# A two-layer graph network on one core: indirect gathers and adding scatters without an upper bound for their indices

## The reference

```
edge_index = jnp.stack([src, dst])        # dst sorted; layer 1: row = src, col = dst
h = jnp.maximum(_layernorm(x), 0.0)
# layer 0
g = (h @ W_embed).reshape(n, H, D)
z = dot(g, a_src)[src] + dot(g, a_dst)[dst];  logit = leaky_relu(z, 0.2)
prob = segment_softmax(logit, dst)
x = x + segment_sum(g[src] * prob, dst) + h @ W_lin + bias
h = jnp.maximum(_layernorm(x), 0.0)
# layer 1
m = relu(concat(h[row], h[col], edge_attr) @ W1 + b1) @ W2 + b2
x = x + h + segment_sum(m * sigmoid(edge_attr @ Wa + ba), row)
```

## Time and profile before

| | |
|---|---|
| median of three runs | 1527.07 us (1523.6 to 1528.55) |
| the profiled execution | 1523.76 us |
| its span in the trace | 1522.0 us |
| GpSimd busy | 1137.3 us, 75% |
| VectorE busy | 1103.2 us, 72% |
| TensorE busy | 1022.8 us, 67% |
| ScalarE busy | 781.4 us, 51% |

### The profile page before, as it was taken

One profiled execution on the slowest core, in us unless ns is written; L12 is line 12 of the kernel. 1 busy time (PEld: TensorE's weight loads), 2 busy tenths in 40 slices (PEclk: granted clock), 3 DMA queues, 4 the chain that ended last, 5 costly groups with the idle time before them and its releaser, 6 DMA issues.

```text
span 1522.0 us, 21349 instructions
## 1 busy us (share of the span) xinstructions
PE 1022.8 (67%) x5699; PEld 766.9 (50%) x5699; DVE 1103.2 (72%) x3789; ACT 781.4 (51%) x2168; POOL 1137.3 (75%) x992
## 2 busy tenths in 40 slices
PE   0877777777778854665554577767777667767774
PEld 0666555555556644555544354544544444445543
DVE  3889898988889897988888655555555555555562
ACT  0788888888888885665665322222222222222221
POOL 5777777777777703777777778888888888888885
PEclk9999999999999986667686688899889889898898
DMA  8477777767677753565554333333333333333332
GB/s 274 124 225 216 223 226 212 241 212 229 211 227 218 219 201 106 178 186 166 171 179 154 102 46 51 51 53 51 50 51 51 53 50 47 52 51 51 51 41 26
DMA packets 177732, 202.55 MB, mean 133 GB/s; under 512 B 22191, under 2 KB 130739, under 8 KB 177483
## 3 DMA queue, kind: packets, MB, share of 16 engines
q1 hardware_dynamic: 119305, 122.62, 25.2%
q0 software_dynamic: 56496, 71.62, 23.7%
q10 hardware_dynamic: 1810, 6.93, 1.3%
HBM read 90.62 MB, written 109.66 MB: 132 GB/s over the span
## 4 chain that ended last, share of the span: by engine, by line
POOL 44%; issue 26%; DMA 16%; DVE 6%; PE 4%; ACT 2%; POOLq 0%; DVEq 0%; ACTq 0%
POOL out_dram L1166 16%; POOL XE L1151 7%; DMA out_dram<-BD,sx 7%; POOL R L434 4%; POOL XN L434 4%; POOL O L434 4%; POOL out_dram L1107 4%; POOL XE L434 4%; DMA XE<-out_dram,ixs 2%; DMA XE<-in_x_dram 2%; DMA out_dram<-BS,sx 1%; DMA out_dram<-BD 1%; DMA O<-in_x_dram,ix 1%; DMA XE<-in_x_dram,ix 1%; DVE H L879 1%
## 5 line engine op out<-in xcount | busy, mean ns | idle before, releaser
L1107 POOL DMA_INDIRECT out_dram<-BD,sx x196 | 206.3, 1053 | 114.1 <-issue 59.4
L1151 POOL DMA_INDIRECT XE<-out_dram,ixs x196 | 210.5, 1074 | 61.8 <-issue 56.7
L1280 DVE TENSOR_SCALAR XN<-bank,bwc 128x128 f32<-128x128 f32 x196 | 55.2, 344 | 260.6 <-PE bank L1420 260.6
L705 ACT ACTIVATE BD<-BD,nmr,rstd 128x128 f32<-128x128 f32 x392 | 170.9, 489 | 63.3 <-DVE nmr L565 63.3
L1046 PE MATMUL bank<-BD 128*128 128x128 f32 x392 | 111.0, 378 | 123.4 <-DVE BD L924 123.4
L1166 POOL DMA_INDIRECT out_dram<-BS,sx x100 | 160.0, 1600 | 37.3 <-issue 33.7
L1166 POOL DMA_INDIRECT out_dram<-TS,sx x96 | 153.1, 1595 | 34.8 <-issue 28.8
L1399 PE MATMUL bank<-ident,XE 128*128 128x128 f32 x196 | 40.9, 344 | 179.5 <-DMA XE<-out_dram,ixs 179.5
L1046 PEld LDWEIGHTS bank<-BD 128*128 128x128 f32 x392 | 87.7, 276 | 134.0 <-issue 134.0
L779 PE MATMUL bank<-wes,TS 128*128 128x132 f32 x392 | 101.3, 342 | 79.3 <-ACT TS L716 78.9
L767 PE MATMUL bank<-ident,BD 128*128 128x128 f32 x588 | 106.3, 292 | 71.7 <-DVE BD L558 69.7
(11 more groups left out here) (238 smaller groups left out, 3222.1 us busy)
## 6 DMA issues: line engine op xcount, KB each, us to landing
out_dram<-BD SPq DMA_DIRECT2D x96, 512.0 KB, 3.1
base_rows<-BD SPq DMA_DIRECT2D x49, 256.0 KB, 4.4
BD<-base_rows SPq DMA_DIRECT2D x49, 256.0 KB, 3.4
H<-BD SPq DMA_DIRECT2D x49, 256.0 KB, 3.0
XE<-in_x_dram SPq DMA_DIRECT2D x13, 512.0 KB
BD<-bond_rows SPq DMA_DIRECT2D x49, 128.0 KB, 2.1
bond_rows<-in_edge_attr_dram ACTq DMA_DIRECT2D x1, 6250.0 KB, 23.5
XN<-in_x_dram SPq DMA_DIRECT2D x12, 512.0 KB
```

What stands on the lines that cost most here:

```text
L705: last = nc.scalar.activation(OT[u][:, g, w:w + D], OT[u][:, g, w + D:w + 2 * D], ACT.Relu, bias=nmr[:, slot, t:t + 1], scale=rstd[:, slot ...
L1107: pool.indirect_dma_start(out, bass.IndirectOffsetOnAxis(sx[:, u, c:c + 1], 0), RO4[u][:, c, :], None, bounds_check=lim, oob_is_err=False) ...
L1151: pool.indirect_dma_start(XS4[u][:, c, :], None, halves, bass.IndirectOffsetOnAxis(ixs[:, u, c:c + 1], 0), bounds_check=lim, oob_is_err=Fa ...
L1280: last = nc.vector.tensor_scalar(MS[:, c * D:(c + 1) * D], bM[:, c * D:(c + 1) * D], bwc[:, u % 2, c:c + 1], None, ALU.mult)
```

## The change

The bound is taken from three kinds of indirect DMA: the gathers of layer 0, the fetches of layer 1 and the adding scatters. Two registers are then no longer filled. The plain scatters keep the bound. Lines behind the first edit move up by one, behind the second by two (L434 becomes L433, L1107 becomes L1106, L1151 becomes L1149 and L1166 becomes L1164).

```diff
         def rows_gpsimd(pool):
-            lim = pool.to_reg(N - 1)
...
                         pool.indirect_dma_start(XA[u][:, c, SRC - s, :], None, x, bass.IndirectOffsetOnAxis(at, 0),
-                                                bounds_check=lim, oob_is_err=False).then_inc(ld_xe[u][c], 16)
+                                                bounds_check=None, oob_is_err=False).then_inc(ld_xe[u][c], 16)
...
         def messages_gpsimd(pool):
-            lim = pool.to_reg(2 * ROWS_OUT - 1)
 
             def fetch(u, c):
                 pool.indirect_dma_start(XS4[u][:, c, :], None, halves, bass.IndirectOffsetOnAxis(ixs[:, u, c:c + 1], 0),
-                                        bounds_check=lim, oob_is_err=False).then_inc(ld_s[u], 16)
+                                        bounds_check=None, oob_is_err=False).then_inc(ld_s[u], 16)
...
                                                 UPD[u][:, c * D:(c + 1) * D], None,
-                                                bounds_check=lim, oob_is_err=True, compute_op=ALU.add).then_inc(ms_add, 16)
+                                                bounds_check=None, oob_is_err=True, compute_op=ALU.add).then_inc(ms_add, 16)
```

## The result

The changed kernel takes 1502.82 us (median of 4 runs, 1502.1 to 1505.48) against 1526.61 us for the kernel before (median of 4 runs, 1523.6 to 1528.55). The ratio is 0.9846, with a 95% interval from 0.9827 to 0.9864. That is faster by 23.8 us, where 53.5 had been forecast. The profiled execution has a span of 1501.1 us, 20.9 less than before; the stages are compared in it.

What follows compares the result with a forecast made beforehand. POOL, issuing indirect DMAs without pause in layer 0 and the messages, was taken as the bound. Savings of 27.4 + 0 + 25.8 + 0.3 = 53.5 us gave 1473 us at the median, range 1420 to 1531 (8 in 10).

Steps and rivals of the forecast that it cites:

- the cover: Layer 0: DVE's floor of 9.3 us a tile lies below POOL's shortened 9.9 us, so POOL's saving shows in the span.
- the first term of the sum: Layer 0: 392 gathers, each 0.07 us shorter without the bound, give 27.4 us.
- The price d: Time of the bound check inside one indirect DMA: 0.07 us likeliest, 0.13 us the end of the likely span.
- Messages: 368 x 0.07 = 25.8 us: Layer 1 messages: 368 adds and fetches on POOL, each 0.07 us shorter, give 25.8 us.
- The copy's loop: Messages: fetched rows through PE to ACT's update copy, which the add needs; 1.7 us of slack per turn of eight DMAs.
- The landing's loop: Messages: an add pair waits until the pair before has landed, 3.24 us after its start; 1.2 us in hand.
- the first fetches: Four fetches of the first batch, on whose landing the first add waits: 0.3 us gained.
- Zero terms: No gain from plain scatters, which keep their bound, or the final drain of 12 adds; the 54.7 us wait before the scatters stays.
- The free check (1): Rival: the check costs nothing in any of the indirect DMAs, time 1524 to 1527 us; chance 0.27.
- The dear check (2): Rival: the check costs 0.15 us or more per indirect DMA, 1415 us at 0.15, not below 1393; chance 0.09.
- A cost of a change of form (3): Rival: the unbounded form costs POOL extra on 764 DMAs, 1555 us at 0.04 us each, 1585 at 0.08; chance 0.06.
- Signs foretold: Profile after: layer 0 step 1.24 us, fetches 0.97 to 1.01, adds 1.50 to 1.55, last gather about 510, messages turn 12.6.

## Why the prediction was right or wrong, point by point

**What bounds the kernel.** POOL, from the first gather to the last fetch: right for the chip of the first measurement. There the gathers' stretch followed their spans with little loss, and the cover was there as said: between 100 and 500 us DVE still waited 29 us for gathered rows, 40 before. It was a reading of one chip at a granted clock of 0.96; at 0.80 POOL waits for DVE and DVE for TensorE, and the first term of the sum is worth nothing.

**The price d.** An eighth of the extra work of an add, 0.07 us, was a guess between 0 and 0.57. Measured it is 0.052 for a gather and 0.067 for a fetch; that the guess came so near for these two is luck, since no row priced a check. Of the 27.4 us for layer 0, 20.4 were there and 17.5 came, since the gathers had more long ones among them (13.4 us instead of 9.3). The direction held and this term was too large by 10 us.

**The adds.** This is the step that failed: "Messages: 368 x 0.07 = 25.8 us". Half of these 368 instructions are adds, and their bound costs nothing, in the changed kernel, alone, and in either mode. That takes 12.9 us off. The prediction had put one d on all three kinds of instruction, though it had just used the add to show that its time is made of something else. No row of the trace could tell what a bound costs in an add, and no reason was given why it should cost the same there.

**The slack.** The two loops that might take the gain away were the right ones, but the slack was read from a single turn. The copy's loop was given 1.7 us, from a turn of the middle class in which the add followed 2.03 us behind the copy, less 0.3. But no add that waited follows its copy by less than 0.83 us, so that turn had 1.2, and the turns of the slow class, 0.85 to 0.95 behind, had about 0.1. The landing's loop was given 1.2 us with the same 0.3; with 0.83 it had 0.7, and the landing of an add does not take 3.24 us each time. The trace of the kernel before already had 7 turns in which POOL waited for landings of 3.8 to 4.0 us, and in the changed one two took over 5. Of 12.3 us that the fetches saved, 4.4 reached the stretch. That is the second failed step, 7.9 us; waits of POOL make 5.5 of them, and most of the rest are the longer first adds, for which the prediction had no term and the runs show no cause.

**The sum.** From 53.5 to 21.0 us of span 32.5 are missing: 9.9 in layer 0, 12.9 for the adds, 0.6 for the size of d in the fetches, 7.9 in the turns, 0.3 for the first fetches, and 0.9 net in between (a later start and a longer wait for DVE, less a shorter way from the first scatter to the first add).

**Zero terms.** The plain scatters stayed at 0.985 us in the median, as a control should; the wait ahead of them stayed at 55 us (56.1); the drain gave nothing.

**The rivals.** The free check (1) is what the adds have, and not the gathers. Of the rule of the Trainium skill, page "DMA: Bandwidth & Descriptors", section "Anatomy of one DMA — SWDGE (gpsimd) path", that the generation of descriptors is small beside about 2 us of fixed cost: in these traces POOL is held for 0.95 to 1.08 us by a gather or fetch, and the landing of a fetch comes at 2.7 us. The trace agrees that the larger part of the latency is elsewhere. It does not follow that less time on POOL is worth nothing, since POOL issues these DMAs one behind the other. The dear check (2) is refuted, 0.05 to 0.07 instead of 0.15. A cost of a change of form (3) is at most 0.008 to 0.009 us where bounded and unbounded gathers alternate, and it has no part in this change, nor is the unbounded form slower; that a fetch behind an add takes 0.05 us more than the next one is as before (1.02 and 0.97 now), and belongs to the operation, not to the bound.

**Signs foretold.** Step 1.24 us: 1.26. Fetches 0.97 to 1.01: 0.97 to 1.02. Adds 1.50 to 1.55: no change, from 1.55 up. Last gather about 510: 520.35. Turn 12.6 us: 13.10 in the mean, 12.80 the shortest.

## What to carry to other kernels

Where GpSimd issues indirect reads of 128 rows back to back, a bound that can't be violated costs 5 to 6% of each instruction's time and can be left out; on plain writes it costs 2%, and on adds nothing. Before a saving is multiplied by a count, ask for each kind of instruction whether it has the cost at all. Read the slack of a loop from its slowest turns, and take off what a waiting engine needs to start (0.83 us here), not the gap that it shows when it doesn't wait (0.30). Read what bounds a stage at the lowest granted clock that the kernel will meet, too: here 17 us of gain in layer 0 became nothing on chips where TensorE was granted 0.79 to 0.84.

## What the runs showed of the hardware

- The price of a bound on 128 indices: 0.052 us for a gather of 512 B rows, 0.067 for a fetch behind adds, 0.02 for a plain write of 512 B rows among fetches, 0 for an add. A gather in the error mode took 0.013 us more than one in the other mode, no more than the same form differs between kernels.
- An adding scatter that had to wait, for a copy on ACT or for a landing, starts no less than 0.83 us behind what it waited for; the gap without a wait is 0.30 us.
- The landing of an add of 128 rows takes 3.4 us in the median, and in the four traces that hold the landings 4 to 9 of 196 take over 4 us, up to 5.1.
- The same program took 1526 us in two sets of runs and 1663 to 1678 us on three other chips, with a granted clock of 0.96 and of 0.79 to 0.84 in layer 0. The instructions of POOL took the same time on both kinds (gathers 0.95 and 1.00 to 1.01 us).
- A chain of TensorE and ACT has three lengths from turn to turn (8.3, 9.9, 10.8 to 11.1 us), at granted clocks of 1.00, about 0.83 and about 0.74 over the stretch.
- Open: why an add hides the check; why single adds land after 5 us, at nearly the same turns in two kernels; why 13 to 25 first adds of turns are long with short fetches and 2 to 9 with bounded ones, but 21 in the kernel before with a matmul less; and why the plain scatters' stage takes 36 us more on the slow chips.
